# Two unread matrix products in twelve slots of an attention and FFN kernel

## The chip, the cores and the metric
The kernel runs on one core of one Trainium2 chip. The metric is the device time of one execution in microseconds (us). Times before are those of three runs, and one further execution was profiled.

## The reference
A block of attention and a gated FFN, each with a residual and a layer norm behind it, on `x` of shape 8 x 512 x 256 in float32. There are 16 heads of 16 features, and the FFN has 1024 hidden features.
```python
q, k, v = x @ Wq.T, x @ Wk.T, x @ Wv.T          # 16 heads of 16
q, k = rope(q), rope(k)
attn = softmax(causal(q @ k.T / sqrt(16)))
x = layernorm(x + (attn @ v) @ Wo.T)
h = silu(x @ w_gate) * (x @ w_up)
h = keep the 2 of each 4 neighbours with the largest magnitude, zero the others
x = layernorm(x + h @ w_down)
```

## The kernel before, in words
Products that need float32's accuracy are split: each operand is a high part (`float32r`) and a low part that holds the rest, and `three_terms` (its matmuls have the line L1062) adds high x high, high x low and low x high.

**Engines.** TensorE is called PE here, VectorE DVE, ScalarE ACT and GpSimd POOL. The order on each is written out by hand. After a prologue for batch 0, all engines walk through slots `g` from `G_FROM = 0` to `G_TO - 1 = 190`. A batch has 20 slots, so batch b has its 20 score steps in slots 20b to 20b + 19, and at each `g` an engine does what is due at that offset of some batch. A table `MISC` gives the offset of each small stage to its batch's first slot: query and key projections ("QK", at -51 to -43), value projections ("V", two at -18 and two at -16), transposes of the heads' outputs ("O", 23 to 27), their second transposes ("aT", 32), the products with Wo ("Wo", 39 and 40) and the transposes of the maxima ("nm", -5). The small stages share three PSUM banks `mi_ps0` to `mi_ps2` in turn. `USES` gives each stage its bank and its number of use, and `start_bank` makes PE wait until the bank's last use has been evacuated (semaphore `mi_ev`).

**A slot on PE**, in this order:
- a fill (up to slot 134): `max_masks` (L1158, four matmuls) and `max_scores` (L1173) put masked scores of the batch after into `mx_ps`. DVE's `block_max` (L900) reduces it to maxima. There is one such buffer, so the masks of the next fill wait for the reduction (`mx_read`).
- `score_step` (L1203) puts transposed scores into `ex_ps`, once ACT has read it. ACT takes the exponential (L751) into `prob0`, `prob13` or `prob2`, and POOL zeroes what causality forbids (L596).
- at slots 5j + 3 and 5j + 6 of a batch `pv_first` and `pv_rest` (both L1220), the probabilities times the values.
- the small stages due at `g`: the projections and Wo at L1062, "O" at L1122, "nm" at L1114, "aT" at L1131.
- from slot 142 on transposes of the first FFN inputs (L1245), and from 147 on the first FFN tiles (`first_tile`, L1268).

In batches up to 4 the slots of a batch hold the QK projections of the batch three later. The last of these (batch 7's) is in slot 97.

**The other engines.** DVE's `normalise` (L926, L928) reads the "O" bank one slot later, `residual` (L941) the Wo bank one slot later, and from slot 141 on DVE splits the FFN weights (L970, L972). These were loaded from slot 122 on. A second part of the program (`ffn_phase`, L1680 to L1734) follows for the rest of the FFN. Ahead of the prologue PE runs `WARM_UP = 40` products that nobody reads (L1292).

Of the kernel before, what the change touches and what calls it, by code (L numbers as in the profile page):

```python
# [12 lines left out]
P = 128  # L13
B, S, D = 8, 512, 256
# [60 lines left out]
LN_AT = [47, 48]  # L75
G_FROM, G_TO = 0, SLOTS * (B - 1) + 51
WARM_UP = 40

# [18 lines left out]
def batch_at(g, at):  # L99

    b, r = divmod(g - at, SLOTS)
    return b if r == 0 and 0 <= b < B else None


def batches_of(g, op, i, later=0):

    return [b for b in range(B) if slot_of(op, b, i) == g - later]
# [7 lines left out]
def misc_at(g):  # L115
    return [(op, b, i) for op, i, _ in MISC for b in batches_of(g, op, i)] + [
        ("X", B - 1, i) for i, at in enumerate(X_AT) if g == SLOTS * (B - 1) + at]


def last_at(g, table):  # L120

    return [n for n, at in enumerate(table) if g == SLOTS * (B - 1) + at]
# [130 lines left out]
def attention_phase(nc, x, xT, wqkvT, woT, cos, sin, ffn_weights, q_parts, k_parts, x1, shared):  # L253
    ctx = ExitStack()
    with ctx:
        def sb(name, shape, dt=f32):
            return ctx.enter_context(nc.sbuf_tensor(name, shape, dt))
# [4 lines left out]
        wqkv_h = sb("wqkv_h", [P, NC, 3 * D], f32r)  # L262
# [107 lines left out]
        def wait_evacuated(engine, op, b, i):  # L370

            bank, use = USES[op, b, i]
            engine.wait_ge(mi_ev[bank], use)
# [18 lines left out]
        def tile_banks(k):  # L392

            return mx_ps if k < RAW or k % 2 == 0 else ex_ps
# [253 lines left out]
        def _(act):  # L648
# [171 lines left out]
            for g in range(G_FROM, G_TO):  # L820
# [13 lines left out]
                for n in last_at(g - 1, [at for _, _, at in TILE_AT]):  # L834
                    part, k, _ = TILE_AT[n]
                    if part == 0 and k < RAW:
                        ev_gate(k)
# [213 lines left out]
        def _(pe):  # L1051
# [13 lines left out]
            def project_qk(b, t):  # L1065
                out = start_bank("QK", b, t)
                if t == 0:
                    pe.wait_ge(x_split, 2 * (b + 1))
                    if b == 0:
                        pe.wait_ge(w_low, 1)  # L1070
                tok, par = slice(P * t, P * t + P), b % 2
                if b == 0:
                    three_terms(out[:], lambda c: xh[par][:, c, tok], lambda c: xl[par][:, c, tok],
                                lambda c: wqkv_h[:, c, 0:2 * D], lambda c: wqkv_l[:, c, 0:2 * D]).then_inc(
                                    made("QK", b, t), 1)
                else:
                    a, odd = divmod(t, 2)
                    features = slice(D * a + odd, D * a + D, 2)
                    three_terms(out[:], lambda c: wqkv_h[:, c, features], lambda c: wqkv_l[:, c, features],
                                lambda c: xh[par][:, c, :], lambda c: xl[par][:, c, :]).then_inc(made("QK", b, t), 1)  # L1080

            def project_v(b, t):
                out = start_bank("V", b, t)
                if b == 0 and t == V_FIRST:
                    pe.wait_ge(w_low, 2)
                tok, par = slice(P * t, P * t + P), b % 2
                three_terms(out[:, 0:D], lambda c: xh[par][:, c, tok], lambda c: xl[par][:, c, tok],
                            lambda c: wqkv_h[:, c, 2 * D:], lambda c: wqkv_l[:, c, 2 * D:]).then_inc(
                                made("V", b, t), 1)

            def transpose_table(i):
                out = start_bank("C", 0, i)
                pe.wait_ge(tables, i + 1)
                for t in range(NT):
                    last = nc.tensor.transpose(out[:, P * t:P * t + P],
                                               table_rows[:, i, t].rearrange("p h i -> p (h i)"), ident[:])
                last.then_inc(made("C", 0, i), 1)
# [12 lines left out]
            def transpose_maxima(b):  # L1110
                out = start_bank("nm", b, 0)
                pe.wait_ge(nm, b + 1)
                for w, t in enumerate(WTILE):
                    last = nc.tensor.transpose(out[0:H, P * t:P * t + P], nmax[:, :, w], ident[:])  # L1114
                last.then_inc(made("nm", b, 0), 1)

            def output_heads(b, t):
                out = start_bank("O", b, t)
                if t == 0:
                    pe.wait_ge(oT_ev, NG * (b + 1))  # L1120
                for j in range(NG):
                    last = nc.tensor.transpose(out[:, P * j:P * j + P], oT_sb[b % 2][:, j, P * t:P * t + P], ident[:])  # L1122
                last.then_inc(made("O", b, t), 1)

            def output_transposes(b, c):
                out = start_bank("aT", b, c)
                if c == 0:
                    for t in range(NT):
                        wait_evacuated(pe, "O", b, t)
                for t in range(NT):  # L1130
                    last = nc.tensor.transpose(out[:, P * t:P * t + P], attn[:, t, P * c:P * c + P], ident[:])  # L1131
                last.then_inc(made("aT", b, c), 1)
# [116 lines left out]
            def first_tile(part, k):  # L1249

                if k == 0 and part == 0:
                    pe.wait_ge(mx_read, FILLS * B)
                    for c in range(NC):
                        wait_evacuated(pe, "X", B - 1, c)
                if k in (0, 4):
                    pe.wait_ge(shared.w_parts, 2 * k + 4 + 4 * part)
                if part == 0 and 0 < k <= RAW + 1 and k != RAW:
                    pe.wait_ge(g_raw, min(k, RAW))
                elif part == 1 and 0 < k <= RAW + 1 and k != RAW:
                    pe.wait_ge(u_raw, min(k, RAW))  # L1260
                elif k == RAW:
                    pe.wait_ge(ex_act, STEPS * B)
                elif k > RAW:
                    pe.wait_ge((shared.silu_s, shared.h_s)[part], k - 1)
                w = (shared.gate, shared.up)[part]
                terms = [(hl, x, c) for c in range(NC) for hl, x in ((0, shared.x1h), (0, shared.x1l), (1, shared.x1h))]
                for n, (hl, x, c) in enumerate(terms):
                    last = nc.tensor.matmul(tile_banks(k)[:, part, :], w[:, hl, c, k, :], x[0][:, c, :], start=n == 0,  # L1268
                                            stop=n == len(terms) - 1)
                last.then_inc((shared.g_done, shared.u_done)[part], 1)  # L1270

            def other(op, b, i):
                if op == "QK":
                    project_qk(b, i)
                elif op == "V":
                    project_v(b, i)
                elif op == "C":
                    transpose_table(i)
                elif op == "nm":
                    transpose_maxima(b)  # L1280
                elif op == "O":
                    output_heads(b, i)
                elif op == "aT":
                    output_transposes(b, i)
                elif op == "X":
                    transpose_x1(i)
                else:
                    output_product(b, i)

            pe.wait_ge(idb_s, 4)  # L1290
            for _ in range(WARM_UP):
                nc.tensor.matmul(mx_ps[:, 0, 0:2 * P], mask_b[:, 0, :], mask_b[:].rearrange("p n k -> p (n k)"),  # L1292
                                 start=True, stop=True)
# [10 lines left out]
            for g in range(G_FROM, G_TO):  # L1304
                b, f = divmod(g - FILL_AT, SLOTS)
                if 0 <= b < B:
                    max_masks(b, f)
                    max_scores(b, f)
                if 0 <= g < SLOTS * B:
                    score_step(g // SLOTS, g % SLOTS)  # L1310
                for j in range(NG):
                    if (b := batch_at(g, 5 * j + PV_FIRST_AT)) is not None:
                        pv_first(b, j)
                    if (b := batch_at(g, 5 * j + PV_REST_AT)) is not None:
                        pv_rest(b, j)
                for op, b, i in misc_at(g):
                    other(op, b, i)
                for n in last_at(g, [at for _, _, at in TILE_AT]):
                    part, k, _ = TILE_AT[n]
                    first_tile(part, k)  # L1320


NK = I // P
# [477 lines left out]
```

## Time and profile before
| | |
|---|---|
| median of three runs | 755.97 us |
| lowest and highest of them | 747.91 and 759.02 us |
| profiled execution | 755.6 us |
| its span, first to last instruction | 753.9 us |
| mean granted TensorE clock | 0.932 of full speed |
| PE busy | 673.1 us, 89% of the span |
| DVE busy | 566.0 us, 75% |
| ACT busy | 412.4 us, 55% |
| POOL busy | 319.5 us, 42% |

Busy shares are means over phases that differ. The attention slots run from about 84 us (first exponential) to 450 us (last), and the FFN phase fills the rest. The granted clock is the share of TensorE's 2.4 GHz that the chip lets through. It shows two levels, 1.00 (2.4 GHz) and 0.50 (1.2 GHz). In the timeline matmuls overlap, so their shown durations are longer than the distance from one to the next.

### The profile page before, as it was taken

To read this page: it belongs to the slowest core of one execution; us is meant where nothing else is said; L and a number is where in the kernel's file an instruction comes from. 1 tells how busy PE (TensorE), PEld (TensorE's weight loads), DVE (VectorE), ACT (ScalarE), POOL (GpSimd) and SP (SyncE) were. 2 spreads that over 40 slices of the span, in tenths; PEclk is the share of its full clock that TensorE was granted. 3 is DMA by queue.
4 is the path that set the end of the run, shared out by engine and by line. 5 is a ranking of instruction groups with operands and counts; after the bars stand their busy time and mean duration, and the time that the engine had idled before them with its cause. 6 is when DMAs were issued, how large, how long until landed. Compare 5 with 4: busy or idle time off the path is not lost. (4 is left out here: it accounts for less than half of the span.)

```text
span 753.9 us, 13714 instructions
## 1 busy us (share of the span) xinstructions
PE 673.1 (89%) x5200; PEld 495.3 (66%) x5200; DVE 566.0 (75%) x822; ACT 412.4 (55%) x583; POOL 319.5 (42%) x314
## 2 busy tenths in 40 slices
PE   6688888999999999988978998399999999999984
PEld 5555554556566565654645566388888898989874
DVE  5497766677677786865755629797989889898975
ACT  5542366576767768664665665453554545353522
POOL 3386478576876777622223322204040404223030
PEclk9797599899999999997989999599999999999996
DMA  4037445445564554542610101300202011010101
GB/s 122 29 78 169 127 139 140 129 123 176 141 170 145 156 169 129 160 142 66 226 57 29 60 2 57 112 28 1 85 0 84 28 56 56 28 56 1 57 0 57
DMA packets 48815, 67.61 MB, mean 90 GB/s; under 512 B 6456, under 2 KB 27448, under 8 KB 48760
## 3 DMA queue, kind: packets, MB, share of 16 engines
q1 hardware_dynamic: 47860, 65.23, 29.5%
q10 hardware_dynamic: 900, 1.64, 0.8%
q8 instruction: 35, 0.57, 0.3%
q14 instruction: 20, 0.16, 0.1%
HBM read 43.12 MB, written 23.07 MB: 88 GB/s over the span
## 5 line engine op out<-in xcount | busy, mean ns | idle before, releaser
L900 DVE TENSOR_REDUCE bmax<-mx_ps 128x8 f32<-128x1024 f32 (+1 forms) x148 | 180.8, 1222 | 90.0 <-PE mx_ps L1173 89.1
L751 ACT ACTIVATE prob<-ex_ps 128x1024 f32<-128x1024 f32 x160 | 164.1, 1025 | 86.4 <-PE ex_ps L1203 82.6
L596 POOL TENSOR_SCALAR_AFFINE_SELECT prob<-prob 128x512 f32<-128x512 f32 x128 | 89.5, 713 | 135.7 <-ACT prob L751 135.7
L1220 PE MATMUL pv_ps<-prob,v_sb 128*32 128x512 f32 (+3 forms) x1024 | 90.4, 476 | 1.6 <-POOL prob L596 1.6
L1158 PEld LDWEIGHTS mx_ps<-mask_b,half_id 64*128 64x128 bf16 x592 | 17.1, 95 | 88.8 <-DVE bmax L900 76.0
L1158 PE MATMUL mx_ps<-mask_b,half_id 64*128 64x128 bf16 x592 | 47.0, 239 | 30.7 <-DVE bmax L900 28.1
L1449 POOL TENSOR_TENSOR hm_l<-v_sb,hm_h 128x2048 fp32r<-128x2048 f32 x4 | 18.5, 4618 | 105.6 <-ACT hm_h L1503 105.6
L1449 POOL TENSOR_TENSOR k_st<-v_sb,q_st 128x2048 fp32r<-128x2048 f32 x4 | 18.8, 4708 | 79.5 <-ACT q_st L1503 79.5
L1220 PEld LDWEIGHTS pv_ps<-prob,v_sb 128*32 128x32 f32 x1024 | 27.6, 116 | 31.2 <-issue 24.9
L1489 ACT ACTIVATE qk_raw<-ex_ps 128x512 f32<-128x512 f32 x28 | 16.6, 591 | 49.5 <-PE ex_ps L1680 49.5
L1173 PE MATMUL mx_ps<-k_st,q_st 48*128 48x512 f32 (+3 forms) x248 | 41.9, 396 | 0.0
L667 ACT ACTIVATE qk_raw<-mi_ps 128x512 f32<-128x512 f32 x32 | 19.2, 599 | 38.4 <-PE mi_ps L1062 33.1
L1489 ACT ACTIVATE qk_raw<-mx_ps 128x512 f32<-128x512 f32 x28 | 16.6, 595 | 42.7 <-PE mx_ps L1680 39.5
L1173 PE MATMUL mx_ps<-w_up_parts,w_gate_parts 48*128 48x128 f32 (+3 forms) x224 | 36.7, 385 | 2.1 <-DVE w_up_parts L881 2.1
L1724 PE MATMUL d_ps<-wd_h,q_st 128*128 128x256 f32 x128 | 36.5, 285 | 0.5 <-DVE k_st L1599 0.4
L1680 PE MATMUL mx_ps<-x1h_odd,w_gate_parts 128*128 128x512 f32 x64 | 23.8, 413 | 14.4 <-DVE wd_l L1558 14.4
L1203 PE MATMUL ex_ps<-q_st,k_st 50*128 50x512 f32 (+3 forms) x256 | 35.4, 335 | 1.1 <-ACT prob L751 1.1
L1724 PE MATMUL d_ps<-wd_l,q_st 128*128 128x256 f32 x128 | 36.2, 283 | 0.0
L1724 PE MATMUL d_ps<-wd_h,k_st 128*128 128x256 f32 x128 | 36.2, 283 | 0.0
L1203 PE MATMUL ex_ps<-w_gate_parts,w_up_parts 50*128 50x512 f32 (+3 forms) x256 | 33.6, 321 | 2.8 <-ACT prob L751 2.7
L425 POOL TENSOR_TENSOR rope_s<-qk_raw,cos_sin 128x512 f32<-128x512 f32 x14 | 17.9, 1280 | 33.8 <-ACT qk_raw L667 33.8
L758 ACT ACTIVATE oT_sb<-pv_ps 128x512 f32<-128x512 f32 x32 | 19.1, 596 | 19.1 <-PE pv_ps L1220 19.1
(253 smaller groups left out, 1992.1 us busy)
## 6 DMA issues: line engine op xcount, KB each, us to landing
y_sb<-x SPq DMA_DIRECT2D x12, 512.0 KB, 4.0
xT_sb<-xT SPq DMA_DIRECT2D x8, 512.0 KB, 4.1
q_st<-q_parts SPq DMA_DIRECT2D x32, 128.0 KB, 2.7
k_st<-k_parts SPq DMA_DIRECT2D x32, 128.0 KB, 2.8
x<-y_sb SPq DMA_DIRECT2D x8, 512.0 KB, 3.3
xh<-x SPq DMA_DIRECT2D x8, 512.0 KB, 4.0
q_parts<-qk_rot SPq DMA_DIRECT2D x14, 256.0 KB, 3.1
k_parts<-qk_rot SPq DMA_DIRECT2D x14, 256.0 KB, 2.8
```

Of the source, the lines that this page charges most:

```text
L596: nc.gpsimd.affine_select(out=block, in_=block, compare_op=ALU.is_ge, fill=0.0, base=0, pattern=[[0, n], [1, P]], channel_multiplier=-1).t ...
L667: nc.scalar.activation(qk_raw[:, t % 2, :], bank_of("QK", b, t)[:], ACT.Copy, scale=0.25 if b > 0 and t < 2 else 1.0).then_inc(evacuated(" ...
L751: nc.scalar.activation(out, ex_ps[:], ACT.Exp).then_inc(ex_act, 1)
L900: nc.vector.tensor_reduce(out=out, in_=src, axis=AX.X, op=ALU.max).then_inc(mx_read, 1)
L1158: nc.tensor.matmul(blocks, half_id[rows, half, :], mask_b[rows, 0:n, 0:P - ROWS * half], start=half == 0, stop=False, skip_group_check=True)
L1173: last = nc.tensor.matmul(fill_banks(b, f)[:, hp, at:at + (qt + 1) * P], q_st[par][rows, hh, P * qt:P * qt + P], k_st[par][rows, hh, 0:(qt ...
L1203: last = nc.tensor.matmul(ex_ps[:, hp, at:at + S - P * kt], k_st[par][rows, hh, P * kt:P * kt + P], q_st[par][rows, hh, P * kt:], start=Tr ...
L1220: last = nc.tensor.matmul(pv_ps[32 * g:32 * g + 32, P * kt:], v_sb[b % 2][:, kt, G4 * j + g, :], probs(g), start=kt == 0, stop=kt == 2, sk ...
L1449: nc.gpsimd.tensor_tensor(hm_l[par][:, 0:4, :], h[0][:], hm_h[par][:, 0:4, :].bitcast(f32), ALU.subtract).then_inc(hm_ls[0], 1)
L1489: nc.scalar.activation(g_sb[:, k % 2, :], g_ps[k % 2], ACT.Silu).then_inc(silu_s, 1)
L1680: last = nc.tensor.matmul(dst[k % 2], w[:, c, k, :], xx[par][:, c, :], start=n == 0, stop=n == 3 * NC - 1)
L1724: last = nc.tensor.matmul(d_ps[t % 2][:, 0:D], hm[par][:, k, tok], w[:, k, :], start=n == 0, stop=n == 3 * NK - 1)
```

## The change
In slots -31, -30, -26, -23, -18, -16, -11, -10, -6, -3, -2 and -1, counted from the first slot of batch 7 (140), PE issues two more products at the end of the slot. These are slots 109, 110, 114, 117, 122, 124, 129, 130, 134, 137, 138 and 139. `keep_busy` looks up the next small stage in a later slot, takes its bank with `start_bank`, so it waits as that stage will for the bank's last reader, and writes 128x512 products of `wqkv_h` into it. They signal no semaphore. The stage that the bank is meant for starts with `start=True` and overwrites them. In slots 122 and 124 the value projections of batch 7 stand ahead of them.
```diff
 WARM_UP = 40
+
+
+IDLE_AT, IDLE = [-31, -30, -26, -23, -18, -16, -11, -10, -6, -3, -2, -1], 2
...
+            def keep_busy(g):
+                op, b, i = next(x for later in range(g + 1, G_TO) for x in misc_at(later))
+                out = start_bank(op, b, i)
+                for _ in range(IDLE):
+                    nc.tensor.matmul(out[:], wqkv_h[:, 0, 0:P], wqkv_h[:, 0, 0:S], start=True, stop=True)
...
                     part, k, _ = TILE_AT[n]
                     first_tile(part, k)
+                if last_at(g, IDLE_AT):
+                    keep_busy(g)
```
No other engine's order changes, and all lines of the file below the table are 3 to 11 lines further down. On PE, slots 108 (its end), 109 and the first part of 110 read before:
```order
L1220 MATMUL pv_ps<-prob0,v_sb1 32x512 x4
L1158 MATMUL mx_ps<-mask_b,half_id 128x2x128 x2
L1158 MATMUL mx_ps<-mask_b,half_id 128x2x64 x2
L1173 MATMUL mx_ps<-w_up_parts,w_gate_parts 128x256 x4
L1203 MATMUL ex_ps<-q_st1,k_st1 128x256 x4
L1158 MATMUL mx_ps<-mask_b,half_id 128x128 x2
```
and now (the names `w_gate_parts` and `w_up_parts` are the memory in which the even batches' `q_st` and `k_st` lie):
```order
L1223 MATMUL pv_ps<-prob0,v_sb1 32x512 x4
L1161 MATMUL mx_ps<-mask_b,half_id 128x2x128 x2
L1161 MATMUL mx_ps<-mask_b,half_id 128x2x64 x2
L1176 MATMUL mx_ps<-w_up_parts,w_gate_parts 128x256 x4
L1206 MATMUL ex_ps<-q_st1,k_st1 128x256 x4
L1279 MATMUL mi_ps0<-wqkv_h 128x512 x2
L1161 MATMUL mx_ps<-mask_b,half_id 128x128 x2
```
The pair stands between the score step and the masks of the next fill, which wait for DVE. Slots 110, 114, 117, 129, 130 and 134 read alike. At the end of slot 124, PE now has the last of the value projections and the pair behind it, on the bank that "O" filled in slot 123 (its row stands first here):
```order
L1125 MATMUL mi_ps1<-ident,oT_sb1 128x128 x4
L1161 MATMUL mx_ps<-mask_b,half_id 128x2x128 x2
...
L1065 MATMUL mi_ps0<-wqkv_l,xh1 128x256
L1065 MATMUL mi_ps0<-wqkv_h,xl1 128x256
L1279 MATMUL mi_ps1<-wqkv_h 128x512 x2
L1161 MATMUL mx_ps<-mask_b,half_id 128x128 x2
```
The masks of slot 125 stood behind the projection and stand behind the pair now. The slots 137 to 139, with no fills, read now:
```order
L1206 MATMUL ex_ps<-w_gate_parts,w_up_parts 128x384 x2
L1206 MATMUL ex_ps<-w_gate_parts,w_up_parts 128x128 x2
L1279 MATMUL mi_ps1<-wqkv_h 128x512 x2
L1206 MATMUL ex_ps<-w_gate_parts,w_up_parts 128x384 x2
L1206 MATMUL ex_ps<-w_gate_parts,w_up_parts 128x128 x2
L1223 MATMUL pv_ps<-prob0,v_sb0 32x512 x4
L1279 MATMUL mi_ps1<-wqkv_h 128x512 x2
L1206 MATMUL ex_ps<-w_gate_parts,w_up_parts 128x256 x4
L1065 MATMUL mi_ps1<-wo_h,aT_h 128x256
```
A pair now stands in front of each of the score steps of slots 138 and 139, and a third behind the twelve matmuls of the Wo product, in front of that of slot 140.

## Rows read from the trace of the kernel before
**Rows 1.** The page's clock row, 40 equal slices of the span, tenths of full speed
```profile
PEclk9797599899999999997989999599999999999996
```
**Rows 2.** Stretches: length, busy us of PE, PEld, DVE, ACT, POOL; clock; DMA
```profile
329.40:334.40 5.00, 2.83 (x34) 1.69 (x38) 3.40 (x5) 3.14 (x5) 1.86 (x3) 1.00 0.58 171
334.40:337.80 3.40, 3.40 (x34) 1.82 (x26) 1.06 (x2) 1.42 (x2) 0.64 (x1) 0.50 0.56 155
...
344.60:354.90 10.30, 8.90 (x64) 4.27 (x64) 4.71 (x5) 4.62 (x6) 1.26 (x3) 0.50 0.18 47
...
382.20:385.60 3.40, 3.40 (x32) 1.63 (x34) 1.02 (x1) 1.62 (x2) 0.64 (x1) 0.50 0.47 154
...
392.40:395.80 3.40, 3.20 (x27) 1.27 (x26) 0.68 (x1) 1.72 (x3) 0.64 (x1) 0.50 0.00 0
...
399.20:402.70 3.50, 3.40 (x19) 2.95 (x16) 0.00 (x0) 1.30 (x2) 1.86 (x3) 0.51 0.02 5
```
**Rows 3.** PE's timeline, masks of slots 106 to 109: start us, us, what
```profile
322.99 0.34 PE L1158 MATMUL mx_ps<-mask_b,half_id 64*128 64x256 bf16 x4
...
325.26 0.26 PE L1158 MATMUL mx_ps<-mask_b,half_id 64*128 64x128 bf16 x4
...
327.37 0.34 PE L1158 MATMUL mx_ps<-mask_b,half_id 64*128 64x256 bf16 x4 [0.72 <-DVE bmax L900]
...
329.38 0.34 PE L1158 MATMUL mx_ps<-mask_b,half_id 64*128 64x256 bf16 x4
```
**Rows 4.** PE's timeline, masks of slots 110 to 113, [idle before <-releaser]
```profile
331.34 0.26 PE L1158 MATMUL mx_ps<-mask_b,half_id 64*128 64x128 bf16 x4 [1.09 <-DVE bmax L900]
...
333.24 0.34 PE L1158 MATMUL mx_ps<-mask_b,half_id 64*128 64x256 bf16 x4 [1.09 <-DVE bmax L900]
...
336.56 0.34 PE L1158 MATMUL mx_ps<-mask_b,half_id 64*128 64x128 bf16 x4
...
338.87 0.34 PE L1158 MATMUL mx_ps<-mask_b,half_id 64*128 64x256 bf16 x4
```
**Rows 5.** PE's timeline, masks of slots 116 to 119
```profile
345.10 0.50 PE L1158 MATMUL mx_ps<-mask_b,half_id 64*128 64x256 bf16 x4 [0.54 <-DVE bmax L900]
...
349.32 0.34 PE L1158 MATMUL mx_ps<-mask_b,half_id 64*128 64x128 bf16 x4
...
351.57 0.50 PE L1158 MATMUL mx_ps<-mask_b,half_id 64*128 64x256 bf16 x4 [0.90 <-DVE bmax L900]
...
354.93 0.34 PE L1158 MATMUL mx_ps<-mask_b,half_id 64*128 64x256 bf16 x4
```
**Rows 6.** PE's timeline, score steps of slots 135 to 141
```profile
391.06 0.49 PE L1203 MATMUL ex_ps<-w_gate_parts,w_up_parts 50*128 50x512 f32 x2 [1.12 <-ACT prob L751]
...
392.67 0.79 PE L1203 MATMUL ex_ps<-w_gate_parts,w_up_parts 50*128 50x512 f32 x2 [0.20 <-ACT prob L751]
...
396.00 0.50 PE L1203 MATMUL ex_ps<-w_gate_parts,w_up_parts 50*128 50x384 f32 x4
397.90 0.51 PE L1203 MATMUL ex_ps<-w_gate_parts,w_up_parts 50*128 50x384 f32 x4 [1.40 <-ACT prob L751]
...
399.53 0.80 PE L1203 MATMUL ex_ps<-w_gate_parts,w_up_parts 50*128 50x256 f32 x4
...
402.94 0.50 PE L1203 MATMUL ex_ps<-q_st,k_st 50*128 50x512 f32 x2
...
404.94 0.50 PE L1203 MATMUL ex_ps<-q_st,k_st 50*128 50x512 f32 x2
```
**Rows 7.** PE's timeline, two products inside the first FFN tile
```profile
420.67 0.40 PE L1268 MATMUL mx_ps<-xl,w_gate_parts 128*128 128x512 f32 x1
420.91 0.63 PE L1268 MATMUL mx_ps<-xh,w_gate_parts 128*128 128x512 f32 x2
```
**Rows 8.** PE's timeline, the masks of slot 125, behind the value projections
```profile
369.13 0.26 PE L1158 MATMUL mx_ps<-mask_b,half_id 64*128 64x128 bf16 x4
```
**Rows 9.** DVE's timeline, division that reads the bank of slot 123
```profile
368.81 0.42 DVE L928 TENSOR_TENSOR attn<-mi_ps,rden 128x256 f32<-128x256 f32 x1
```

## Prediction
> **What bounds the kernel now.** I read the clock row of the 40-slice table first, then the busy table over the stretches between clock changes, then the timeline of TensorE (PE) inside and outside them. The clock row [rows 1] shows nothing but 9s for slices 9 to 18, the middle of the attention phase, and then a 7 in slice 19 and an 8 in slice 21, about 339 to 358 and 377 to 396 us, in the second half of batch 5 and of batch 6. The stretches [rows 2] make that exact: from 329.4 to 334.4 us PE was busy 2.83 of 5.00 us at granted clock 1.00 (2.4 GHz), and from 334.4 to 337.8 it is granted 0.50 (1.2 GHz). The same level is granted for 344.6 to 354.9, 382.2 to 385.6, 392.4 to 395.8 and 399.2 to 402.7. That is five stretches and 24.0 us. In these PE is busy nearly all the time (3.40 of 3.40, 8.90 of 10.30), so here the slow clock sets the pace, while just before them PE had been waiting.
>
> For what it was waiting, the timeline says. In a plain slot the four masks of the next maximum fill start 1.90 us after the last ones, and 1.09 us of that is a wait for VectorE's reduction of `mx_ps` (the row at 331.34 and the step to 333.24) [rows 4]. So a plain slot is bound by the one buffer `mx_ps` going round PE and VectorE, not by PE's work. In batches up to 4 the same slots hold projections of a later batch. In the last two no query or key projection is left. After slot 134 no fills are left either, and PE waits for the exponential on ScalarE: 1.12 us at 391.06 and 1.40 us at 397.90 [rows 6].
>
> **What the slow clock costs.** I take slot lengths from start to start at full clock and subtract. With `pv_rest`: 322.99 to 325.26, 2.27 us. With `pv_first`: 327.37 to 329.38, 2.01 us [rows 3]. Plain: 331.34 to 333.24, 1.90 us [rows 4].
> First stretch: slot 111 runs 333.24 to 336.56, 3.32 us for 2.27, and slot 112 2.31 us (336.56 to 338.87) for 1.90. 1.05 + 0.41 = 1.45 us [rows 4].
> Second, the long one: slot 116 takes 4.22 us for 2.27, slot 117 2.25 for 1.90, slot 118 3.36 for 2.01. 1.95 + 0.35 + 1.35 = 3.65 us [rows 5].
> Third (382.2): the same slots of the next batch and as long as the first [rows 2], so 1.45 us.
> Fourth and fifth: slot 136 runs 392.67 to 396.00, 3.33 us, for at most 2.27 (it has no fill), 1.05 us; slot 139, a score step and a Wo product, runs 399.53 to 402.94, 3.41 us, where slot 140 with the same work at full clock takes 2.00 (402.94 to 404.94): 1.40 us [rows 6]. Together 2.45 us.
> The sum is 1.45 + 3.65 + 1.45 + 2.45 = 9.0 us. This is what the clock can give back in batches 5 and 6, the upper bound of the gain. The lower bound is nothing.
>
> **What the products cost.** The nearest operation in the trace is the FFN tile of the same shape, 128x512 on 128 rows: from 420.67 to 420.91, 0.24 us at full clock [rows 7]. Two are 0.47 us, and at 1.2 GHz twice that, 0.95 us. They write only a small-stage bank and signal nobody, so what they can delay is what stands behind them on PE: the masks and fill of the next slot, hence VectorE's reduction, and the next score step, hence ScalarE's exponential.
> Eight of the twelve pairs have cover. Slots 109, 110, 129, 130 and, at full clock, 117 have about 1.09 us of waiting for VectorE in front of the next masks [rows 4]; slot 114 is followed by a like wait (its row is of the same kind); slot 134 has 1.12 us of waiting for ScalarE and slot 137 1.40 us [rows 6]. 0.47 us fits in each, and even 0.95 us does, just. They cost 0.
> Four have none. Slots 122 and 124 do hold projections, the value projections of batch 7, and behind them the next masks start at once: the row at 369.13 has no idle time [rows 8]. Slot 138 ends with `pv_first` and slot 139 with the Wo product, and the score steps behind them (399.53, 402.94) start without a wait [rows 6]. 4 x 0.47 = 1.9 us.
> The pairs also wait for the bank of the next small stage. In eleven slots its last reader is several slots gone. In slot 124 it is the bank that `output_heads` filled in slot 123, and VectorE's division reads it until 368.81 + 0.42 = 369.23 us [rows 9], where PE would otherwise go on at 369.13 [rows 8]. So PE waits some 0.15 us there, with the masks of slot 125 behind it. The products cost 1.9 + 0.15 = 2.05 us in all. Between 0.5 us (all four stalls partly swallowed by the round trips behind them) and 5.7 us (24 x 0.24, no cover at all) is the range of that term. The four uncovered slots are read directly, so I take 2.05.
>
> **Does it reach the end?** By the program's order VectorE's residual of batch 5 and its splitting of the FFN weights stand behind the Wo products of slots 139 and 140, and PE's first FFN tiles in the slots from 147 on. Both come earlier by what is saved, and no row shows anything between that is fixed in time, so I let the whole pass to the end.
>
> **A rule against the change.** The rows show the clock falling after a stretch in which PE was busy 2.83 of 5.00 us and never waited longer than 1.09 us at a time [rows 2, 4]. The Trainium skill, page "TensorE: Matmul & The Clock Gate", section "Why this matters for your kernels", puts falls mid-kernel down to long pauses between bursts of matmuls and asks only that there be none. The trace disagrees: there is no such pause here. Were the rule the whole story, filling short waits would buy nothing and only the 2.05 us would be left. The same page's section "A second HAM failure mode: psum-queue depth-cycling" says that frequent micro-idles between groups can make the clock swing too. The trace agrees with this second rule, and by it the change acts as in my sum.
>
> **The rivals.**
> The slow stretches move instead of going. The pairs stand in only some of the waiting slots: between 111 and 117, and around 135 and 136, PE still waits, and the clock may fall one slot later and meet a `pv_rest` again. For it speaks that slots 135 and 136 lie behind each other with waits on ScalarE and only one pair ahead of them; against it that all plain slots in front of the five falls get a pair. Half of the 9.0 us is then gained: 4.5 - 2.05 = 2.45 us, so 753.5 us.
> More goes than I count. What follows moves by some 7 us against the clock's changes, and the one slow stretch of batch 7 or the restart in the FFN phase may come out shorter by two terms of the size of the first, 2.9 us: 746.1 us. As likely they come out longer, which is in my range.
> Slower than before. The clock falls as it does now and the pairs stay. Then all four uncovered pairs cost their price, that of slot 139 the price at 1.2 GHz (0.95 for 0.47), and in slot 117 a pair of 0.95 us meets a wait of 0.90 us (the row at 351.57) [rows 5]. 2.05 + 0.5 + 0.05 = 2.6 us, so 758.6 us. The place is the masks behind slots 122, 124, 138 and 139. It decides as soon as less than 2.05 us is won from the clock, that is, if only one short stretch goes. For it speaks that nothing in this trace shows the clock being held by such a filler; against it that the same slots with projections in them, as at 355 to 382 us, run at full clock.
> That the change doesn't do what it says: it is in part so, as slots 122 and 124 do have projections. That is in the sum.
>
> **How the numbers follow.** The profiled execution took 755.6 us (span 753.9 and 1.7 around it). 755.6 - 9.0 + 2.05 = 748.7 us. It lies 0.4 us under the median of the three runs, 755.97, so the forecast is 749.0 us. The three runs lie 11 us apart (747.91 to 759.02), wide for one kernel, and the clock's changes falling differently on the slots would do that; a median of three may therefore be off by 3 us for that alone. Chances: forecast 0.5, stretches move 0.25, more goes 0.1, slower 0.15. The forecast's own range is 745 to 753. For 8 in 10 I go from 743.5 (more goes, and a few us of scatter) to 757.5, which takes in the movers and part of the slower case. 2% is 15 us, about what a measurement of this kernel can tell from no change, and all the slow stretches together give 9.0. So faster by over 2% 0.03, within 2% 0.95, slower by over 2% 0.02.
>
> **What would show it.** Right: a clock row with 9s in slices 19 and 21, slots 111, 116, 131 and 136 near 2.3 us from start to start, pairs of about 0.47 us at the new line with the wait before the next masks shorter by as much in the plain slots, and the first FFN tile some 7 us earlier than in the trace of before (the tile's rows at 420.67 and on) [rows 7]. The step behind the cover is wrong if plain slots grow beyond 1.9 to 2.0 us. The step on the bank is wrong if PE waits in slot 124 much over 0.15 us. The forecast is wrong if 1.2 GHz is still granted for about 20 us between 330 and 405 us, or if the first tile is earlier but the end is not.

## The result and the profile after

The changed kernel takes 747.01 us (median of 4 runs, 745.80 to 747.82) against 756.87 us (4 runs, 747.91 to 759.02). The ratio is 0.9893 with a 95% interval of 0.9848 to 0.9938, 1.1% less time. The profiled execution took 747.09 us, span 745.4.

The page's clock row of the changed kernel, 40 equal slices in tenths of full speed, to be laid beside [rows 1]:
```profile
PEclk9887799899999999999998999699999999999996
```
The 7 and the 8 of slices 19 and 21 are 9s now. The first slices, in front of any changed instruction, differ too, and that matters for how two profiles are compared.

The same is seen in numbers over the stretch from the exponential of slot 111 to that of slot 141, which begins and ends with the same instruction in both kernels. First the kernel before, then the changed one (length, busy us of PE, PEld, DVE, ACT, POOL, granted clock, DMA):
```profile
334.20:405.50 71.30, 61.96 (x570) 37.32 (x573) 40.29 (x54) 40.36 (x51) 16.67 (x28) 0.83 0.33 106
```
```profile
332.70:396.60 63.90, 58.20 (x590) 35.24 (x594) 40.28 (x54) 40.47 (x50) 16.67 (x28) 1.00 0.36 118
```
DVE, ACT and POOL do the same work to within 0.2 us. PE has 20 more matmuls recorded and is yet busy 3.8 us less, as the granted clock is 1.00 where it was 0.83. The stretch is 7.4 us shorter.

The ends of that stretch, on ScalarE's timeline, before and after:
```profile
334.20 1.02 ACT L751 ACTIVATE prob<-ex_ps 128x1024 f32<-128x1024 f32 x1 [0.98 <-PE ex_ps L1203]
405.49 1.02 ACT L751 ACTIVATE prob<-ex_ps 128x1024 f32<-128x1024 f32 x1 [0.98 <-PE ex_ps L1203]
```
```profile
332.72 1.02 ACT L754 ACTIVATE prob<-ex_ps 128x1024 f32<-128x1024 f32 x1 [0.98 <-PE ex_ps L1206]
396.61 1.02 ACT L754 ACTIVATE prob<-ex_ps 128x1024 f32<-128x1024 f32 x1 [0.97 <-PE ex_ps L1206]
```
They give 71.29 and 63.89 us, 7.40 less. They also show that slot 111 came 1.48 us earlier (332.72 for 334.20) in an execution whose program is the same up to slot 109. This part of the 8.5 us between the two spans is not the change: in the prologue and in batch 0 the clock fell at other moments (slices 2 to 8 of the two clock rows). The rest of the difference: 8.5 = 7.40 + 1.48, less 0.11 in slots 141 to 151 and 0.27 behind slot 159.

The slots that stood at 1.2 GHz, on PE's timeline of the changed kernel (masks of slots 111 to 113 and 116 to 119; these answer to [rows 4] and [rows 5]):
```profile
330.60 0.73 PE L1279 MATMUL mi_ps<-wqkv_h 128*128 128x512 f32 x2
331.77 0.34 PE L1161 MATMUL mx_ps<-mask_b,half_id 64*128 64x256 bf16 x4 [0.44 <-DVE bmax L903]
...
334.04 0.26 PE L1161 MATMUL mx_ps<-mask_b,half_id 64*128 64x128 bf16 x4
...
335.94 0.34 PE L1161 MATMUL mx_ps<-mask_b,half_id 64*128 64x256 bf16 x4
...
342.17 0.34 PE L1161 MATMUL mx_ps<-mask_b,half_id 64*128 64x256 bf16 x4 [0.56 <-DVE bmax L903]
...
344.44 0.26 PE L1161 MATMUL mx_ps<-mask_b,half_id 64*128 64x128 bf16 x4
...
346.33 0.34 PE L1161 MATMUL mx_ps<-mask_b,half_id 64*128 64x256 bf16 x4 [0.43 <-DVE bmax L903]
...
348.34 0.34 PE L1161 MATMUL mx_ps<-mask_b,half_id 64*128 64x256 bf16 x4
```
Slot 111 takes 2.27 us (331.77 to 334.04) where it took 3.32, slot 116 2.27 for 4.22, slot 117 1.89 for 2.25, slot 118 2.01 for 3.36. The wait for VectorE in front of the masks of slot 111 is 0.44 us where it was 1.09: the pair stands in the wait and the masks are no later.

The score steps of slots 135 to 140, which answer to [rows 6]:
```profile
384.14 0.50 PE L1206 MATMUL ex_ps<-w_gate_parts,w_up_parts 50*128 50x512 f32 x2 [0.46 <-ACT prob L754]
...
385.75 0.51 PE L1206 MATMUL ex_ps<-w_gate_parts,w_up_parts 50*128 50x512 f32 x2 [0.20 <-ACT prob L754]
...
387.62 0.50 PE L1206 MATMUL ex_ps<-w_gate_parts,w_up_parts 50*128 50x384 f32 x4
...
389.51 0.50 PE L1206 MATMUL ex_ps<-w_gate_parts,w_up_parts 50*128 50x384 f32 x4 [0.73 <-ACT prob L754]
...
391.60 0.50 PE L1206 MATMUL ex_ps<-w_gate_parts,w_up_parts 50*128 50x256 f32 x4
...
394.07 0.50 PE L1206 MATMUL ex_ps<-q_st,k_st 50*128 50x512 f32 x2
```
Slot 136 takes 1.87 us (385.75 to 387.62) for 3.33. Slot 139 takes 2.47 (391.60 to 394.07) for 3.41: the Wo product is back at full clock and the uncovered pair is paid for behind it.

### The profile page after: what moved, and what is told of

Same layout as the page of the kernel before. It is cut to its first block and busy times, and to the rows that moved or that the text cites. A ratio compares the mean times of both kernels' runs of the same rounds, so it can differ in the third digit from the quotient of the medians.

```text
span 745.4 us, 13762 instructions
## 1 busy us (share of the span) xinstructions
PE 672.5 (90%) x5224; PEld 495.5 (66%) x5224; DVE 565.5 (76%) x822; ACT 412.7 (55%) x583; POOL 318.5 (43%) x314
## 5 line engine op out<-in xcount | busy, mean ns | idle before, releaser
L1223 PE MATMUL pv_ps<-prob,v_sb 128*32 128x512 f32 (+3 forms) x1024 | 84.7, 450 | 0.6 <-POOL prob L599 0.6
L1223 PEld LDWEIGHTS pv_ps<-prob,v_sb 128*32 128x32 f32 x1024 | 26.1, 111 | 28.1 <-issue 22.5
L1176 PE MATMUL mx_ps<-k_st,q_st 48*128 48x512 f32 (+3 forms) x248 | 40.3, 382 | 0.0
L1206 PEld LDWEIGHTS ex_ps<-q_st,k_st 50*128 50x128 f32 x256 | 23.1, 193 | 8.6 <-issue 5.1
```

The costliest lines, as they stand in the source:

```text
L1176: last = nc.tensor.matmul(fill_banks(b, f)[:, hp, at:at + (qt + 1) * P], q_st[par][rows, hh, P * qt:P * qt + P], k_st[par][rows, hh, 0:(qt ...
L1206: last = nc.tensor.matmul(ex_ps[:, hp, at:at + S - P * kt], k_st[par][rows, hh, P * kt:P * kt + P], q_st[par][rows, hh, P * kt:], start=Tr ...
L1223: last = nc.tensor.matmul(pv_ps[32 * g:32 * g + 32, P * kt:], v_sb[b % 2][:, kt, G4 * j + g, :], probs(g), start=kt == 0, stop=kt == 2, sk ...
```

## The experiments

All are edits of the changed kernel. Each ran beside the kernel before on one chip, and its ratio is to those runs. "Section" is the time from one exponential's start to another's in the profiled execution. The profiles differ by up to 4 us before any changed instruction (the exponential of slot 111 starts between 330.09 and 334.20 us), and what stands behind the exponential of slot 159, the same in all, takes 302.7 to 305.2 us. So sections tell more than spans.

**The waits without the products.**
```diff
-IDLE_AT, IDLE = [-31, -30, -26, -23, -18, -16, -11, -10, -6, -3, -2, -1], 2
+IDLE_AT, IDLE = [-31, -30, -26, -23, -18, -16, -11, -10, -6, -3, -2, -1], 0
```


> The products are left out and only the waits for the bank stay in the twelve slots. Theory A (the products keep the clock up): with no products the clock falls as in the kernel before, 20 us or more at 1.2 GHz between 330 and 405 us after allowing for a shift, slots 111 to 140 take as long as before (about 69.3 us from exponential 111 to 140), and the time is 755 to 758 us. Rival B (the added waits or the mere shift of PE's queue space the slots differently and the clock's changes then miss the long products): the time stays at 745 to 750 us.


Measured: 754.25 us (10 runs, 752.09 to 756.64), ratio 1.0007 (0.9972 to 1.0042) to a median before of 755.18. Its stretches at 1.2 GHz, as in [rows 2]:
```profile
327.80:332.80 5.00, 2.56 (x34) 1.63 (x30) 3.25 (x5) 3.23 (x5) 1.86 (x3) 1.00 0.53 157
332.80:336.20 3.40, 3.40 (x32) 1.41 (x32) 1.23 (x1) 1.30 (x2) 0.64 (x1) 0.50 0.62 158
343.00:349.80 6.80, 6.61 (x50) 3.24 (x48) 3.36 (x4) 3.18 (x5) 0.63 (x1) 0.50 0.29 80
380.60:384.00 3.40, 3.40 (x34) 1.82 (x26) 0.99 (x2) 1.45 (x2) 0.64 (x1) 0.51 0.43 144
390.80:394.20 3.40, 3.39 (x26) 1.28 (x26) 0.68 (x1) 1.45 (x2) 0.63 (x1) 0.50 0.02 5
397.60:404.40 6.80, 6.59 (x32) 5.60 (x29) 1.45 (x3) 2.24 (x3) 1.86 (x3) 0.50 0.00 0
```
All five are there, 23.5 us of them between slots 111 and 141 (23.9 before), and that section takes 72.2 us (71.3 before). So the products make the gain in that section, and with the waits alone no gain is seen in the time. The first two rows show again what a fall looks like: 2.56 of 5.00 us busy ahead of it, and then PE busy throughout at half speed. One thing did change with the waits alone: the ten runs span 4.6 us, where the 19 runs of the kernel before beside them span 10.6. I have no cause for that.

**No pairs behind the value projections.**
```diff
-IDLE_AT, IDLE = [-31, -30, -26, -23, -18, -16, -11, -10, -6, -3, -2, -1], 2
+IDLE_AT, IDLE = [-31, -30, -26, -23, -11, -10, -6, -3, -2, -1], 2
```


> The pairs of slots 122 and 124, behind the value projections, are left out. Theory A: these two had no cover and guard nothing, since projections stand there; slots 122 and 124 shorten by 0.48 and 0.81 us, clock unchanged: 747.0 - 1.3 = 745.7 us. Rival B (they are part of what keeps the clock up in batch 6): a stretch at 1.2 GHz comes back between 355 and 385 us, and the time is 747 to 749 us.


Measured: 744.54 us (4 runs, 743.96 to 746.24), ratio 0.9872 (0.981 to 0.9934). Section 121 to 131 takes 21.65 us where the changed kernel takes 22.93: 1.28 us less, at full clock. No stretch at 1.2 GHz came back behind them: with two products elsewhere, the two pairs bought nothing and cost 1.3 us. In the profiled execution the clock fell once in batches 5 and 6, from 342.0 to 345.4 us, in slot 116, which takes 3.77 us for 2.27. No pair had been taken away ahead of that: the program up to there is that of the changed kernel, in whose two profiles the clock stays up. So two products in the plain slots do not keep the clock up there in every execution.

**Only the first four slots.**
```diff
-IDLE_AT, IDLE = [-31, -30, -26, -23, -18, -16, -11, -10, -6, -3, -2, -1], 2
+IDLE_AT, IDLE = [-31, -30, -26, -23], 2
```


> Only the pairs of slots 109, 110, 114 and 117 stay. Theory A (each stretch is removed by the pairs just ahead of it): the stretches at 334 and 345 us are gone and slots 111 to 119 are 5.1 us shorter than before, those at 382, 392 and 399 us stay or move by a few us; 756.9 - 5.1 = 751.8 us. Rival C (the clock remembers a longer past, or the alignment decides): batch 6 keeps its clock too, and the time is 747 to 749 us, or batch 5 loses it again.


Measured: 748.84 us (10 runs, 745.50 to 751.99), ratio 0.9925 (0.9893 to 0.9957). Section 111 to 121 takes 21.30 us, as in the changed kernel (21.27; 26.39 before): 5.1 us less, as expected. In batch 6 the clock falls again, in the slots left bare:
```profile
366.00:371.10 5.10, 3.59 (x40) 1.89 (x40) 3.50 (x6) 4.02 (x7) 1.85 (x3) 1.00 0.21 69
371.10:378.00 6.90, 5.91 (x46) 3.27 (x47) 2.88 (x3) 2.87 (x4) 0.63 (x1) 0.51 0.31 105
384.80:388.20 3.40, 3.40 (x30) 1.47 (x28) 0.68 (x1) 1.56 (x3) 0.63 (x1) 0.50 0.03 5
391.60:395.00 3.40, 3.40 (x15) 2.74 (x15) 0.62 (x1) 1.02 (x1) 1.33 (x3) 0.50 0.00 0
```
So the effect is local: each stretch goes with the pairs just ahead of it, and nothing carries over from batch 5 to batch 6. The time is 3 us under the 751.8 expected. A part of that is the base: the median of the kernel before beside these runs was 755.2, not 756.9, and 755.2 - 5.1 = 750.1. For the last 1.3 us I have no cause that is shown. The profile cannot give it: section 111 to 141 is only 4.24 us shorter than before, and another 4.1 us lie ahead of slot 109, where nothing was changed.

**One product for two.**
```diff
-IDLE_AT, IDLE = [-31, -30, -26, -23, -18, -16, -11, -10, -6, -3, -2, -1], 2
+IDLE_AT, IDLE = [-31, -30, -26, -23, -18, -16, -11, -10, -6, -3, -2, -1], 1
```


> One product for two in each of the twelve slots. Theory A with a margin: one is enough in most plain slots, uncovered cost halves (2.05 to 1.0 us), 746.0 us. Theory A without a margin: one is too little in the slots with the longest waits (109, 110, 129, 130 and 134 to 138), one to three of the five stretches come back at 1.45 us or more each, 748 to 751 us. Rival B (spacing by waits, not products): as the changed kernel, 747 us.


Measured: 743.66 us (4 runs, 741.70 to 748.04), ratio 0.9883 (0.981 to 0.9955). In the profiled execution (741.7 us) there is no fall at all from slot 111 to the end of the attention slots, not in batch 7 either, and section 111 to 141 takes 62.98 us: 0.91 less than with two, which is the uncovered cost, halved (0.24 in slot 122, 0.23 in each of 124, 138 and 139). Its runs reach up to 748.04 though, with granted clocks from 0.945 to 0.961, so it seems to differ from run to run whether one is enough.

**Four products for two.**
```diff
-IDLE_AT, IDLE = [-31, -30, -26, -23, -18, -16, -11, -10, -6, -3, -2, -1], 2
+IDLE_AT, IDLE = [-31, -30, -26, -23, -18, -16, -11, -10, -6, -3, -2, -1], 4
```


> Four products for two in each of the twelve slots, 0.95 us a time. By the cost model: in the plain slots 109, 110, 129 and 130 0.95 us still fits before the reduction is read (the wait left before the masks falls from 0.43 to about 0), these slots stay at 1.9 us; slots 122, 124, 138 and 139 grow by 0.47 us each over the changed kernel, 1.9 us, and slot 134 and 137 by up to 0.2 us; clock as in the changed kernel. 747.0 + 2.1 = 749.1 us. Rival (a product is never hidden, each costs its 0.23 us): 747.0 + 24 x 0.23 = 752.5 us.


Measured: 747.55 us (6 runs, 745.49 to 748.52), ratio 0.991 (0.9873 to 0.9948). Slots 110 and 111 on PE's timeline:
```profile
331.31 1.20 PE L1279 MATMUL mi_ps<-wqkv_h 128*128 128x512 f32 x4
332.47 0.34 PE L1161 MATMUL mx_ps<-mask_b,half_id 64*128 64x256 bf16 x4
```
Four fill the wait, which is gone from the row of the masks, and the slot still takes 1.90 us (330.57 to 332.47). Section 111 to 121 is 21.29 us, as with two. The uncovered slots grow by 0.45, 0.47, 0.47 and 0.47 us (slots 122, 124, 138 and 139), and section 111 to 141 takes 65.81 us, 1.92 more than the changed kernel, against 1.9 expected. Each product costs its 0.23 us where there is no cover, and nothing where there is. The median is 1.5 us under the 749.1 expected. In the profile the unchanged part behind slot 159 took 302.96 us, 2.0 less than in the changed kernel, with less time at 1.2 GHz in it, so the sections bear the cost model out and the median doesn't test it.

**One product, none behind the value projections.**
```diff
-IDLE_AT, IDLE = [-31, -30, -26, -23, -18, -16, -11, -10, -6, -3, -2, -1], 2
+IDLE_AT, IDLE = [-31, -30, -26, -23, -11, -10, -6, -3, -2, -1], 1
```


> One product, and none in slots 122 and 124. Theory A: the run with one product kept the clock up everywhere in batches 5 and 6, so this takes from it only the uncovered cost of the two slots, 0.24 + 0.6 us: 743.7 - 0.8 = 742.9 us, no stretch at 1.2 GHz longer than 3.4 us between 330 and 400 us. Rival: one product without margin, a stretch or two come back (as slots 134 to 138 are the thinnest), 745 to 747 us.


Measured: 748.04 us (12 runs, 742.30 to 752.15), ratio 0.9909 (0.9879 to 0.9938). The expectation was missed by 5 us. The rival was right in kind, and the median lies 1 us above its 745 to 747. The runs spread over 10 us with clocks from 0.939 to 0.963. Even the profiled one, the fastest (742.3 us), has a fall at 381.7 to 385.1 us. One product is not enough in every run. That it did better in the experiment with all twelve slots (743.66) may be its four runs. It isn't settled whether the pairs behind the value projections help there.

**Batch 7 too.** As the one before, with pairs in batch 7. The pairs of slots 142, 144 and 145 go to `mx_ps`, which nobody uses between slot 134 and slot 147.
```diff
-IDLE_AT, IDLE = [-31, -30, -26, -23, -18, -16, -11, -10, -6, -3, -2, -1], 2
+IDLE_AT, IDLE = [-31, -30, -26, -23, -11, -10, -6, -3, -2, -1], 1
+LATE_MX_AT, EARLY_MX_AT = [2, 4], [5]
...
+            def keep_busy_mx():
+                pe.wait_ge(mx_read, FILLS * B)
+                for _ in range(2):
+                    nc.tensor.matmul(mx_ps[:, 0, :], wqkv_h[:, 0, 0:P], wqkv_h[:, 0, 0:S], start=True, stop=True)
...
                     score_step(g // SLOTS, g % SLOTS)
+                if last_at(g, EARLY_MX_AT):
+                    keep_busy_mx()
...
                     keep_busy(g)
+                if last_at(g, LATE_MX_AT):
+                    keep_busy_mx()
```


> As the kernel with one product and none in slots 122 and 124, and two products each at the end of slots 142 and 144 and between score step and small stages of slot 145, into mx_ps, which nobody uses there. Theory A: the one stretch at 1.2 GHz in batch 7 (404 to 411 us, where slots 145 to 147 take 2 to 3 us more) goes, and exponential 141 to 147 takes about 13.0 us in place of 14.5 to 14.7: 1.5 us less than the kernel without them wherever that has the stretch, 741.5 us. Rival: the wait there is for VectorE and GpSimd (the splitting of the FFN weights) and the time stays at 743 us though the clock stays up.


Measured: 747.74 us (7 runs, 745.68 to 750.48), ratio 0.9915 (0.9884 to 0.9947). The section from 141 to 147 takes 14.27 us where 13.0 was expected: the fall is there, at 411.4 us. It starts behind the longest wait of PE in batch 7, which the timelines of PE and of GpSimd show:
```profile
408.75 0.50 PE L1207 MATMUL ex_ps<-q_st,k_st 50*128 50x512 f32 x2
410.85 2.34 PE L1224 MATMUL pv_ps<-prob,v_sb 128*32 128x384 f32 x24 [1.60 <-POOL prob L600]
```
```profile
406.12 0.81 POOL L619 TENSOR_SCALAR vare<-meanvar 128x4 f32<-128x4 f32 x1
407.01 1.04 POOL L621 TENSOR_TENSOR rstd<-vare,mhalf 128x4 f32<-128x4 f32 x1
408.13 0.58 POOL L623 TENSOR_TENSOR mrstd<-meanvar,rstd 128x4 f32<-128x4 f32 x1
408.80 1.01 POOL L625 TENSOR_SCALAR mrstd<-mrstd 128x4 f32<-128x4 f32 x1
409.77 2.35 POOL L600 TENSOR_SCALAR_AFFINE_SELECT prob<-prob 128x512 f32<-128x512 f32 x2
```
In slot 146 PE waits 1.60 us for masks that stand behind four small operations of the layer norm on GpSimd. I had filled the slots in front of that wait and not the wait itself. That this lets the clock fall is not shown. In the profile with one product in twelve slots nothing fills batch 7, the same wait is there, and the clock stays up (section 141 to 147 takes 13.21 us):
```profile
404.51 1.50 PE L1223 MATMUL pv_ps<-prob,v_sb 128*32 128x384 f32 x24 [1.59 <-POOL prob L599]
```

**Batch 0 too.** The diff is against the one before.
```diff
-IDLE_AT, IDLE = [-31, -30, -26, -23, -11, -10, -6, -3, -2, -1], 1
+IDLE_AT, IDLE = [-140, -139, -128, -121, -120, -31, -30, -26, -23, -11, -10, -6, -3, -2, -1], 1
```


> As the one before, and one product each in slots 0, 1, 12, 19 and 20 of batches 0 and 1. Theory A (any plain slot that only waits for mx_ps profits alike): the stretch near 130 us goes, exponential 19 to 23 takes about 8.3 us in place of 11.2, and the stretch at 84 us shortens by up to 1.5 us; about 3 us less than the one before, 738.5 us. Rival: one product a slot is too little there or the fall comes a slot later, no gain, 741.5 us.


Measured: 744.37 us (6 runs, 741.96 to 749.48), ratio 0.9878 (0.9836 to 0.992). Section 19 to 23 takes 8.69 us (11.22 in the one before): 2.5 us less, and the fall near 130 us is gone. But the stretch at 84 us, expected to shorten, is longer in this profile (75.9 to 92.9 us, where there were two of 6.9 and 3.4 us), section 0 to 19 takes 0.88 us more, and section 0 to 30 is only 1.66 us shorter. The median is 3.4 us under the 747.74 of the one before. That is near the 3 us expected, though the runs of the two overlap (741.96 to 749.48 and 745.68 to 750.48). Both medians lie 6 us above what was written. Both have one product, and both profiles have three falls in batches 5 and 6.

**The changed kernel once more.** No edit.


> The changed kernel once more, to be compared on one chip with the two below and to see its spread. Theory A: 746 to 748 us, with a spread of some 5 us less than the kernel before, whose runs differ by 10 us, since fewer slots are left in which the clock may fall. Rival: its four runs so far were close together by luck, and the spread is as wide as that of the kernel before.


Measured: 746.62 us (6 runs, 744.66 to 747.86), ratio 0.9892 (0.9854 to 0.9929). The ten runs of the two measurements span 3.2 us. The 11 runs of the kernel before beside the last six span 8.7 (748.88 to 757.60).

**Batch 7 filled, two products.**
```diff
-IDLE_AT, IDLE = [-31, -30, -26, -23, -18, -16, -11, -10, -6, -3, -2, -1], 2
+IDLE_AT, IDLE = [-31, -30, -26, -25, -23, -11, -10, -6, -3, -2, -1], 2
+LATE_MX_AT, EARLY_MX_AT = [2, 4], [5, 6, 6]
...
-                if last_at(g, EARLY_MX_AT):
+                for _ in last_at(g, EARLY_MX_AT):
```
(The last two lines are against the kernel of "Batch 7 too", and `keep_busy_mx` is as there.)


> Pairs (two products) without those of slots 122 and 124, one pair more in slot 115, and into mx_ps a pair each at the end of slots 142 and 144, one between score step and small stages in slot 145 and two such in slot 146, which waits 1.60 us for GpSimd. Theory A: the stretches of batches 5, 6 and 7 are all gone; sections (exponential to exponential) 111 to 121 about 21.3, 121 to 131 21.65, 131 to 141 19.7, 141 to 151 23.0 us. Against the changed kernel 1.3 us from the value slots and 1.5 from batch 7: 744.2 us. Rival: the pairs in batch 7 delay what VectorE and GpSimd wait for, and section 141 to 151 stays at 24.5 us: 745.7 us.


Measured: 743.51 us (6 runs, 741.84 to 745.77), ratio 0.9853 (0.9815 to 0.9892). Sections 111 to 121, 121 to 131, 131 to 141 and 141 to 151 take 21.28, 21.65, 19.69 and 23.02 us, all as written, and the median is 3.1 us under that of the changed kernel beside it. The 1.5 us of batch 7 are not shown to come from the filler, as a profile without it had 22.98 us in section 141 to 151. Of the eleven profiles in which some of batch 7's waits are unfilled, ten have a fall there, and the two with all filled have none. The clock is 1.00 throughout (the stretch over batches 5 to 7, same columns as above):
```profile
331.00:415.00 84.00, 77.71 (x741) 46.78 (x742) 60.41 (x88) 54.83 (x70) 27.01 (x40) 1.00 0.33 105
```

**Batches 0 and 7.** The diff is against the one before.
```diff
-IDLE_AT, IDLE = [-31, -30, -26, -25, -23, -11, -10, -6, -3, -2, -1], 2
+IDLE_AT, IDLE = [-140, -139, -128, -121, -120, -31, -30, -26, -25, -23, -11, -10, -6, -3, -2, -1], 2
```


> As the one before, and pairs in slots 0, 1, 12, 19 and 20 as well. Theory A: exponential 0 to 30 takes 67.0 us or less (68.7 with the clock falling near 130 us), 2 to 2.5 us less than the one before: 742 us. Rival: what is gained in slots 19 to 23 is lost in slots 0 and 1, where the clock is at 1.2 GHz already and a pair costs 0.95 us: 744 us.


Measured: 741.0 us (6 runs, 738.06 to 742.75), ratio 0.982 (0.978 to 0.9859). Section 0 to 30 takes 65.94 us (68.70 in the changed kernel), and section 0 to 19 is no longer (41.82 for 42.10), so the rival is out. Its clock row has only 9s from slice 6, where batch 0's slots have begun, to slice 25, in front of the FFN phase:
```profile
PEclk9886899999999999999999999799999999999998
```
And slot 146, PE's wait for GpSimd shortened from 1.60 to 0.47 us by the filler, at full clock (`pv_rest` behind it takes 1.50 us, not 2.34):
```profile
402.30 1.20 PE L1285 MATMUL mx_ps<-wqkv_h 128*128 128x512 f32 x4
403.96 1.50 PE L1224 MATMUL pv_ps<-prob,v_sb 128*32 128x384 f32 x24 [0.47 <-POOL prob L600]
```
This version beats both kernels: 5.6 us less than the changed one beside it, with its slowest run (742.75 us) under that one's fastest (744.66), and 14 us less than the kernel before.

## Why the prediction was right

749.0 us was predicted, 747.01 measured, inside the range of 743.5 to 757.5 and inside the likeliest case's own 745 to 753. The mechanism was right: with the products the five stretches go, and with the waits alone they come back. That the sum comes out so close is in part luck, as its errors go both ways. The clock gave 0.63 us more than predicted, the products cost 0.17 more, and 0.38 us were lost behind slot 141, which together is 7.03 us saved for 6.95. The other 1.5 us between the two profiles lie ahead of the change. The terms:

- The clock, 9.0 us. First stretch 1.45 predicted: exponential 111 to 113 is 1.46 us shorter. Second 3.65: exponential 113 to 121 is 3.66 shorter. Third 1.45: 1.62. Fourth and fifth 2.45: slots 135 and 136 are 1.48 shorter and slot 139 0.94 with its pair, so 1.41 without. This is 2.89, more than the 2.45, because I priced slot 136 with a yardstick that held a fill, and it has none (1.87 us, not 2.27). In all 9.63.
- The products, 2.05 us. Slot 122 grows by 0.48 and slot 124 by 0.81 us (0.47 and 0.62 were predicted), slot 138 by 0.46 (1.63 to 2.09 from score step to score step) and slot 139 by 0.47. That is 2.22. The mis-sized part is the wait for the bank in slot 124:
```profile
363.16 0.73 PE L1279 MATMUL mi_ps<-wqkv_h 128*128 128x512 f32 x2
363.82 0.26 PE L1161 MATMUL mx_ps<-mask_b,half_id 64*128 64x128 bf16 x4
```
```profile
362.68 0.42 DVE L931 TENSOR_TENSOR attn<-mi_ps,rden 128x256 f32<-128x256 f32 x1
```
  The division is done at 363.10 and the pair starts at 363.16. The last projection matmul started at 362.79, and without the wait the pair would have followed it 0.12 us later, as in slot 122, at 362.91. So PE waited 0.25 us where I had "some 0.15". My rows gave neither number: 369.23 - 369.13 is 0.10, and 369.13 is where the masks start, while the pair follows the last projection 0.12 us behind its start (368.92 + 0.12 = 369.04), which gives 0.19. And from the pair's start to the masks it is 0.66 us here, behind the pause, and 0.56 in slot 122 (357.59 to 358.15). I had not counted this 0.10.
- 9.63 - 2.22 = 7.41 us against the 7.40 measured between exponentials 111 and 141, and 6.95 predicted. The eight covered pairs cost nothing, as the 0.44 us left of the 1.09 us waits shows. The experiment with four products confirms it with twice the length.
- That it reaches the end: of the 7.40 us 7.0 are left in the span (0.11 lost in slots 141 to 151, 0.27 behind them). The first FFN tile came 8.73 us earlier (411.94 for 420.67), of which 1.48 lie ahead of the change. The stretch of batch 7 moved from 416.3 to 404.4 us and doubled to 6.9 us, for only 0.1 us. PE is busy in nearly all of it, but the slowed transposes and scores in front of `pv_rest` of slot 146 ran into PE's wait for GpSimd, which shrank from 1.59 to 0.60 us. Before, then the changed kernel's two rows and its stretch (columns as above):
```profile
416.63 2.79 PE L1220 MATMUL pv_ps<-prob,v_sb 128*32 128x384 f32 x24 [1.59 <-POOL prob L596]
```
```profile
407.76 2.79 PE L1223 MATMUL pv_ps<-prob,v_sb 128*32 128x384 f32 x24 [0.60 <-POOL prob L599]
411.94 0.39 PE L1271 MATMUL mx_ps<-xl,w_gate_parts 128*128 128x512 f32 x1
```
```profile
404.40:411.30 6.90, 6.23 (x39) 3.44 (x40) 6.70 (x14) 2.06 (x3) 3.87 (x5) 0.51 0.19 68
```
- The medians differ by 9.9 us, more than the 7.4. The four runs of the kernel before stood high: its three larger sets of runs have medians of 755.0 to 755.2, 8.0 to 8.6 us above the changed kernel's two medians. What is left over 7.0 may be falls that vary by run; it isn't shown.
- The rivals: that the stretches move instead of going did not happen in the changed kernel's two profiles. It is not ruled out for two products, as one of the six profiles with two or more in the plain slots of both batches has a fall in batch 5 (342.0 us, without the value slots). With one product three of four profiles have falls in batches 5 and 6, and the median without the value slots is 748.04 us. The slower case, in which the clock falls as before and the pairs cost, did not occur in any profile with products. I gave it 0.15 for want of any row of a filler that holds the clock. With the waits alone the falls came back.
- No wait of PE in batches 5 and 6 of the kernel before was longer than 1.46 us, and filling waits of that kind took all five falls away in the changed kernel. The longest is that behind slot 114:
```profile
343.20 0.26 PE L1158 MATMUL mx_ps<-mask_b,half_id 64*128 64x128 bf16 x4 [1.46 <-DVE bmax L900]
```
  The Trainium skill, page "TensorE: Matmul & The Clock Gate", section "Why this matters for your kernels", asks for no long idle pauses between bursts of matmuls, so that throughput doesn't drop mid-kernel. As the whole rule that fails here: there was no such pause, and the clock fell five times. The Trainium skill's section "A second HAM failure mode: psum-queue depth-cycling" on the same page tells of a kernel in which TensorE idled briefly and often between groups and the clock swung. The traces of the kernel before and of the waits alone agree with it.

## What to carry to other kernels

Where an engine pair goes round one buffer and TensorE waits a microsecond in each turn, look at the granted clock behind such slots. Here the slots with the waits kept their length, and what was won lay in the next dense stretch, which had run at half speed. In this kernel unread products inside waits that were read from the trace cost nothing, and those behind work that ends on time cost their full length (0.23 us each), so place them by the idle time of the next instruction's row. Compare profiles by sections between two like instructions, since executions of this kernel differ by up to 4 us before the first changed one.

## What the runs showed of the hardware that I had not expected

- The time of a run goes with its mean granted clock. The kernel before took 757.32 us at 0.928, 755.03 at 0.932, 753.32 at 0.941 and 748.79 at 0.950, about 3.9 us for each 0.01. It is a trend and not an order: at 0.943 alone its runs lie between 749.68 and 752.60 us. The scatter of 10 us is thus for the most part a scatter in how long the clock stays down. The changed kernel's ten runs span 3.2 us. That filling the waits is what narrows it is not shown, as the ten runs with the waits alone span 4.6 us.
- The fastest case and the safest are not the same: one product a slot gave the fastest single execution of the first four variants (741.7 us), and without the value slots the widest spread of all variants (742.3 to 752.15 us).
- A fall costs little where the slowed work stands in front of a wait: 6.9 us at 1.2 GHz in batch 7 of the changed kernel cost 0.1 us more than 3.4 us had, as the slowed work in front took 1.0 us out of the wait for GpSimd. The 3.4 us themselves cost 1.4 (section 141 to 151 takes 24.43 us, and 23.0 without a fall).
